# The first quad of self-attention: rows of x first on the load queue, weights in four pieces, normalisation ahead of the weight splits

## What is computed

```python
xn = layernorm(x)                       # per token, over 256
xq, xk, xv = xn @ wq.T, xn @ wk.T, xn @ wv.T      # 256 -> 1024 each
scores = softmax(xq.reshape(b, 16, s, 64) @ xk.reshape(b, 16, s, 64).T / 8)
x = x + (scores @ xv.reshape(b, 16, s, 64)) @ wo.T
```

## Time and profile before

| | |
|---|---|
| three runs | 1566.71, 1567.07 and 1562.39 us, median 1566.71 |
| the profiled execution | 1566.04 us, span 1564.3 us |
| time of it outside the span | 1.7 us |
| TensorE busy | 1434.1 us, 92% of the span |
| first matmul (transpose) of the span | 20.72 us |
| first projection matmul | 23.89 us |
| mean granted TensorE clock | 0.967 |

### The profile page before, as it was taken

One profiled execution on the slowest core, in us unless ns is written; L12 is line 12 of the kernel. 1 busy time (PEld: TensorE's weight loads), 2 busy tenths in 40 slices (PEclk: granted clock), 3 DMA queues, 4 the chain that ended last, 5 costly groups with the idle time before them and its releaser, 6 DMA issues. The chain is left out here.

```text
span 1564.3 us, 40213 instructions
## 1 busy us (share of the span) xinstructions
PE 1434.1 (92%) x12305; PEld 1241.7 (79%) x12305; DVE 967.4 (62%) x2473; ACT 763.7 (49%) x1879; POOL 682.0 (44%) x1060
## 2 busy tenths in 40 slices
PE   4999999999999999789999999999999369999997
PEld 3888878888888888668888888888887258888886
DVE  5747575757565656357777777777775235555553
ACT  4647474747464656236655655655655112222221
POOL 5434353535353535512355455465464523333332
PEclk9999999999999999789999999999999579999999
DMA  5606060707070707077667767767764235554451
GB/s 191 136 5 167 20 172 13 179 9 181 8 177 11 173 12 176 26 217 194 193 176 198 194 178 195 194 176 196 195 168 141 69 110 166 197 194 169 160 191 54
DMA packets 181964, 218.31 MB, mean 140 GB/s; under 512 B 83838, under 2 KB 150309, under 8 KB 181638
## 3 DMA queue, kind: packets, MB, share of 16 engines
q1 hardware_dynamic: 176360, 208.56, 48.1%
q0 software_dynamic: 3968, 6.59, 1.3%
q10 hardware_dynamic: 1568, 2.30, 0.5%
HBM read 138.67 MB, written 80.48 MB: 140 GB/s over the span
## 5 line engine op out<-in xcount | busy, mean ns | idle before, releaser
L1431 DVE TENSOR_REDUCE row_max<-psb_s 100x1 f32<-100x361 f32 x512 | 265.3, 530 | 140.1 <-PE psb_s L1654 135.0
L1305 ACT ACTIVATE probs<-psb_t 121x400 f32<-121x400 f32 (+1 forms) x384 | 190.4, 507 | 89.7 <-PE psb_t L1664 82.8
L1654 PE MATMUL psb_s<-k,q 97*100 97x362 f32 x512 | 185.0, 363 | 12.8 <-DVE row_max L1431 4.9
L519 POOL TENSOR_TENSOR diag<-neg_ident,row_max 100x400 fp32r<-100x400 f32 x128 | 112.8, 903 | 175.5 <-DVE row_max L612 146.7
L1664 PE MATMUL psb_t<-q,k 98*121 98x200 f32 (+1 forms) x768 | 148.5, 276 | 1.8 <-ACT probs L1305 1.8
L2144 PE MATMUL psd_h<-h_in,w_sb 128*128 128x256 f32 x640 | 144.0, 384 | 1.4 <-ACT h_in L2010 1.4
L2152 PE MATMUL psd_y<-w_sb,hid 128*128 128x256 f32 x640 | 144.5, 379 | 0.0
L2144 PEld LDWEIGHTS psd_h<-h_in,w_sb 128*128 128x128 f32 x640 | 123.3, 193 | 18.9 <-issue 1.8
L2152 PEld LDWEIGHTS psd_y<-w_sb,hid 128*128 128x128 f32 x640 | 120.1, 190 | 15.5
L1664 PEld LDWEIGHTS psb_t<-q,k 98*121 98x121 f32 (+1 forms) x768 | 126.8, 186 | 5.6 <-ACT probs L1305 2.5
L2025 ACT ACTIVATE hid<-psd_h,b_sb 128x256 f32<-128x256 f32 x100 | 47.4, 474 | 148.5 <-PE psd_h L2144 147.2
(11 more groups left out here) (230 smaller groups left out, 3710.0 us busy)
## 6 DMA issues: line engine op xcount, KB each, us to landing
w_sb<-in_w SPq DMA_DIRECT2D x40, 1024.0 KB, 7.6
routed_rows<-empty SPq DMA_DIRECT2D x7, 3855.0 KB, 18.7
packed_keys<-k_st SPq DMA_DIRECT2D x32, 724.0 KB, 4.1
k<-packed_keys SPq DMA_DIRECT2D x64, 362.0 KB
v_rows<-v_tok SPq DMA_DIRECT2D x32, 400.0 KB
v_ext<-v_rows SPq DMA_DIRECT2D x32, 400.0 KB
q<-packed_queries SPq DMA_DIRECT2D x64, 200.0 KB
k<-packed_keys SPq DMA_DIRECT2D x64, 181.0 KB
```

The lines of the kernel that those rows point to most:

```text
L519: pool.tensor_tensor(diag[:, g % 2], c.neg_ident[0:S, 0:S].unsqueeze(1).to_broadcast([S, GH, S]), row_max[:, g // 2 % 2, g % 2].unsqueeze( ...
L1305: act.activation(probs[0:KT[kt], u % 2, kt], ps_t[i % 2][0:KT[kt], 0:4 * S], ACT.Exp, scale=HD2 ** -0.5).then_inc(probs_ready, 1)
L1431: dve.reduce_max(row_max[:, p, h:h + 1], ps_s[h % 2][0:S, 0:S2], AX_X).then_inc(max_ready, 1)
L1654: pe.matmul(ps_s[h % 2][0:S, 0:S2E], q2[0:97, p, u, g, S * a:S * (a + 1)], k2[0:97, p, u, g], start=True, stop=True).then_inc(scores_ready, 1)
```

## The change

The diff below leaves nothing out but the mechanical replacement of the semaphores' names and counts for `wvT` and `woT` (their two low parts become four, one for each half). `piece_loaded[0]` and `[1]` are used again for `wvT` and `woT`.

```diff
+        PIECES = [(qk, half) for half in range(2) for qk in range(2)]
+        def columns(w, qk, half):
+            return w[:, qk, :, O1 // 2 * half:O1 // 2 * (half + 1)]
 # SP
             load_x(0, x_first)
-            sp.wait_ge(w_loaded[0], 16)
+            for n, (qk, half) in enumerate(PIECES):
+                first = O1 * qk + O1 // 2 * half
+                sp.dma_start(columns(w_stage, qk, half), wqkT[:, first:first + O1 // 2].rearrange(
+                    "(k p) n -> p k n", p=128)).then_inc(piece_loaded[n], 16)
             load_x(1, x_second)
             for i, w in ((2, wvT), (3, woT)):
-                sp.wait_ge(w_lo_ready, i - 1)
+                sp.wait_ge(w_lo_ready, i + 1)
 # ACT
-            for i, w in enumerate((wqkT[:, 0:O1], wqkT[:, O1:2 * O1])):
-                act.dma_start(w_stage[:, i], w.rearrange("(k p) n -> p k n", p=128)).then_inc(w_loaded[i], 16)
-            for i in range(2):
-                act.wait_ge(w_loaded[i], 16)
-                act.copy(w_hi[:, i], w_stage[:, i]).then_inc(w_hi_ready, 1)
+            def high_bits(n):
+                act.wait_ge(piece_loaded[n], 16)
+                act.copy(columns(w_hi, *PIECES[n]), columns(w_stage, *PIECES[n])).then_inc(w_hi_ready, 1)
+            high_bits(0)
+            high_bits(1)
             leading_bits(0)
+            high_bits(2)
+            high_bits(3)
 # POOL
-                pool.tensor_copy(w_hi[:, n + 2], w_stage[:, n]).then_inc(vo_hi_ready, 1)
-                pool.wait_ge(vo_hi_ready, n + 1)
-                pool.tensor_tensor(w_lo[:, n + 2], w_stage[:, n], w_hi[:, n + 2].bitcast(F32),
-                                   ALU.subtract).then_inc(vo_lo_ready, 1)
+                for half in range(2):
+                    hi, lo, src = columns(w_hi, n + 2, half), columns(w_lo, n + 2, half), columns(w_stage, n, half)
+                    pool.tensor_copy(hi, src).then_inc(vo_hi_ready, 1)
+                    pool.wait_ge(vo_hi_ready, 2 * n + half + 1)
+                    pool.tensor_tensor(lo, src, hi.bitcast(F32), ALU.subtract).then_inc(vo_lo_ready, 1)
 # DVE
+            def low_bits(n):
+                dve.wait_ge(w_hi_ready, n + 1)
+                hi, lo, src = (columns(t, *PIECES[n]) for t in (w_hi, w_lo, w_stage))
+                dve.tensor_tensor(lo, src, hi.bitcast(F32), ALU.subtract).then_inc(w_lo_ready, 1)
             moments(0)
-            low_bits(0)
             for i in range(QUAD):
                 normalize(0, i)
-            low_bits(1)
+            low_bits(0)
             trailing_bits(0)
+            for n in range(1, len(PIECES)):
+                low_bits(n)
 # PE
-                pe.wait_ge(xn_ready, q * QUAD + QUAD)
+                if not isinstance(q, int):
+                    pe.wait_ge(xn_ready, q * QUAD + QUAD)
                 for k in range(KD):
                     for i in range(QUAD):
+                        if isinstance(q, int) and k == 0:
+                            pe.wait_ge(xn_ready, q * QUAD + i + 1)
                         ins = pe.transpose(...)
+                if isinstance(q, int) and q == 0 and t % 4 == 0:
+                    pe.wait_ge(w_lo_ready, t // 2 + qk + 1)
-                    if f == FV and isinstance(q, int) and q == 0:
-                        pe.wait_ge(vo_lo_ready, 1)
+                    if f in (FV, FV + 1) and isinstance(q, int) and q == 0:
+                        pe.wait_ge(vo_lo_ready, f - FV + 1)
             turn_x(0)
-            pe.wait_ge(w_lo_ready, 2)
```

More of the change, by code:

```diff
@@ L202, in self_attention @@
         x_loaded = sem("x_loaded")
-        w_loaded = [sem(f"w_loaded{i}") for i in range(4)]
+        PIECES = [(qk, half) for half in range(2) for qk in range(2)]
+        piece_loaded = [sem(f"piece_loaded{n}") for n in range(len(PIECES))]
         w_hi_ready = sem("w_hi_ready")
@@ L313, in _ @@
             load_x(0, x_first)
-            sp.wait_ge(w_loaded[0], 16)
+            for n, (qk, half) in enumerate(PIECES):
+                first = O1 * qk + O1 // 2 * half
+                sp.dma_start(columns(w_stage, qk, half), wqkT[:, first:first + O1 // 2].rearrange(
+                    "(k p) n -> p k n", p=128)).then_inc(piece_loaded[n], 16)
             load_x(1, x_second)
             for i, w in ((2, wvT), (3, woT)):
-                sp.wait_ge(w_lo_ready, i - 1)
+                sp.wait_ge(w_lo_ready, i + 1)
                 sp.dma_start(w_stage[:, i % 2].rearrange("p k n -> p (k n)").rearrange(
                     "p (k n) -> p k n", n=w.shape[1]), w.rearrange("(k p) n -> p k n", p=128)
-                             ).then_inc(w_loaded[i], 16)
+                             ).then_inc(piece_loaded[i - 2], 16)
             for q in range(2, QUADS):
@@ L349, in cross_inputs @@
             def cross_inputs():
-                sp.wait_ge(vo_lo_ready, 2)
+                sp.wait_ge(vo_lo_ready, 4)
                 for dst, src in ((c.wk_st, cross["wk"]), (c.wv_st, cross["wv"]), (c.wq_sb, cross["wq"])):
@@ L439, in quad @@
                         if isinstance(q, int) and q == 0 and r - 2 < 2:
-                            act.wait_ge(vo_lo_ready, 2)
+                            act.wait_ge(vo_lo_ready, 4)
                         else:
@@ L469, in split_weights @@
             def split_weights(n):
-                pool.wait_ge(w_loaded[n + 2], 16)
-                pool.tensor_copy(w_hi[:, n + 2], w_stage[:, n]).then_inc(vo_hi_ready, 1)
-                pool.wait_ge(vo_hi_ready, n + 1)
-                pool.tensor_tensor(w_lo[:, n + 2], w_stage[:, n], w_hi[:, n + 2].bitcast(F32),
-                                   ALU.subtract).then_inc(vo_lo_ready, 1)
+                pool.wait_ge(piece_loaded[n], 32)
+                for half in range(2):
[3 more added lines that the diff above has]
+                    pool.tensor_tensor(lo, src, hi.bitcast(F32), ALU.subtract).then_inc(vo_lo_ready, 1)
             inverse_root(0)
@@ L479, in _ @@
             split_weights(1)
-            pool.wait_ge(vo_lo_ready, 2)
+            pool.wait_ge(vo_lo_ready, 4)
             pool.memset(c.mask_t, 0).then_inc(c.cross["mask_cleared"], 1)
@@ L779, in quad @@
                             if isinstance(q, int) and q == 0:
-                                pe.wait_ge(vo_lo_ready, 2)
+                                pe.wait_ge(vo_lo_ready, 4)
                             hi, lo = (t[:, i % 2] for t in (o_hi, o_lo))
```

## The result

The changed kernel takes **1557.01 us** (median of 11 runs, 1551.37 to 1560.1) against 1565.12 us for the kernel before, run beside it (11 runs, 1561.84 to 1567.48). The ratio is 0.9947, 95% interval 0.9932 to 0.9962: 8.1 us less, with an interval of about 6 to 10.6 us. The forecast was 1558.5 us (7.5 less). The profiled execution took 1555.15 us, span 1553.4.

A forecast was written before the change was run, and what follows sets the result against it. The late landing of x was taken to bound the kernel's start: first projection 8.3 us earlier, 0.8 given back before the fifth, so 7.5 us off the profiled 1566.04, giving 1558.5 us; 8-in-10 range 1554.5 to 1564.5.

The forecast's parts named there:

- The bound: Kernel start: x, 0.4 MB, not the 2 MB of weights, bounds it; issued first, x lands at 8.2 us, not 13.83.
- Statistics to the first projection: From x's landing: var_eps at 10.3, xn done 13.1, x_lo 15.45, first projection 15.6 us, 8.3 earlier than 23.89.
- The 1.84 us: Start, on POOL: without low_bits(0) beside it, var_eps takes 0.23 us instead of 2.07, which removes 1.84 us by itself.
- From the first projection to the fifth: Three low_bits on DVE delay the copies; fifth projection at 22.65 us (before 30.14), giving back 0.8 of 8.3 us.
- wvT, woT and POOL: Value fills: wvT's second half ready by 29.7 to 30.7, needed at 31.9 us; margin 1.2 us or more, no cost.
- The other margin: Next quad: POOL's inverse_root(1) ends at 38.2 to 40.3 us, DVE's normalize wants it at 41.3; 1 us left at worst.
- Rival B: POOL becomes the bound at the second value fill or next normalize: 3 to 5 us lost, 1562 to 1563 us; chance 0.10.
- The pieces and wvT: Weight loads: pieces 0 and 1 land by 11.1, needed by 12.7; wvT waits until 18.05 and lands at 23.1 us.
- The sum: Whole kernel: 8.3 - 0.8 = 7.5 us gained from the profiled 1566.04 us, giving 1558.5 us, 0.48% less.
- Rival A: Start: x lands at 11 to 13.8 us, not 8.2; 2.8 to 5.6 us lost, 1561.3 to 1564.1 us; chance 0.13.
- Rival C: First stage: new breaks keep TensorE at its low clock, up to 22 us lost, 1570 to 1578 us; chance 0.05.
- Rival D: Two later changes of stage: clock levels fall otherwise, 1561.5 to 1566 us despite full gain at the start; chance 0.10.

The follow-up runs named there:

- experiment 2: Kernel before, with both whole weight loads moved from ACT's queue to SP's, behind x; order of work unchanged: 1561.21 us, ratio 0.9973.
- experiment 4: Changed kernel, with the four weight pieces issued on ACT's queue beside x on SP's, second quad of x waiting for piece 1: 1556.09 us, ratio 0.9945.
- experiment 5: Changed kernel, but SP issues the weight pieces only when x has landed: 1557.05 us, ratio 0.9960.
- experiment 1: Kernel before, loads kept: normalize ahead of low_bits(0), low_bits(1) behind trailing_bits, transposes batch by batch: 1563.63 us, ratio 1.0002.
- experiment 6: Changed kernel with low_bits(0) put back ahead of normalize: 1560.37 us, ratio 0.9957.
- Experiment 7: Changed kernel plus 105 small warming matmuls (ratio 1.0034), 30 wide ones (0.9954), low parts of pieces 2 and 3 on POOL (0.9963), or the last two together (0.9960).
- the last experiments: Changed kernel plus wide warming matmuls and low parts of pieces 2 and 3 on POOL: 1556.28 us; with loads issued beside the constants too: 1553.51 us.

## Why the prediction was right

*The bound.* "x, 0.4 MB, is the bound of the start": experiments 2, 4 and 5 show it. x landed at 8.27 where the sum said 8.2. Alone, the load took 4.12 us against the 4.4 of the sum of 2.5 us that don't depend on size and 1.9 at the rate of the later x loads; the total is measured, the split between the two terms is not.

*Statistics to the first projection.* `var_eps` 10.41 (10.3), `xn` done 13.19 (13.1), `x_lo` done 15.49 (15.45), first projection 15.54 (15.6). The 1.84 us that the prediction ascribes to taking `low_bits(0)` from beside `var_eps` is real with the old loads: in experiment 1 `var_eps` took 0.24 us and not 2.07. With x early and pieces of half the size the same order is worth less, 0.9 us, and by way of `rstd` (experiment 6). The sum did not hang on it, since it added up the new order from its own start.

*From the first projection to the fifth.* Forecast 0.8 us given back, measured 0.43. The copies started at 18.92 and not at 19.2, since three `low_bits` took 3.49 us and not 3.6. That this stretch is paced by DVE was half the truth. The prediction had TensorE done with its four banks "by 21.5 to 23, depending on the clock", but counted only DVE's 22.65. Experiment 7 shows the lower clock as a second bound at nearly the same place, and in three kernels with the same work here it ended last and put the fifth projection 0.3 to 0.45 us later than in the changed one. That the profiled execution of the changed kernel had an early rise is luck, of that size.

*wvT, woT and POOL.* No wait of TensorE at the value fills, as forecast. The second half of wvT was ready at 29.72 (27.33 + 2.39), and the second value fill started at 31.78: 2.1 us of margin where I had 1.2 or more. The other margin, 1 us at worst, was 2.3: the next quad's `rstd` was ready at 38.55, and DVE's first `xn` started at 40.87. Rival B did not happen, and the last experiments show how near it is: with the fills 2.0 us earlier it takes more than half of the gain.

*The pieces and wvT.* Piece 1 landed at 11.18 (11.1), due at 12.7; wvT was issued at 17.78 (18.05) and landed at 22.75 (23.1).

*The sum.* 7.5 us forecast; 7.92 at the fifth projection, 8.0 at `diag`, 8.1 in the medians. Of the 1.5 us between the forecast time, 1558.5, and the measured one, 0.6 are the gain and 0.9 the base: the forecast counted from an execution of 1566.04 us, and the median beside the changed kernel was 1565.12. That the whole sum came within 0.6 us is partly luck, since neither the marks nor the medians are that sharp. Rival A (x not early) is refuted by the landing at 8.27. Rival C (the clock) did not happen; the weight loads were at the higher level from 19.4 us on. Rival D, the later stages falling otherwise, is there with a spread of 8 us, in either direction, and not only at the two changes of stage: up to 5 us of it lie within self-attention. It did not carry the median away.

## What to carry to other kernels

When a load is late, look at what was issued beside it and not only at its size: the small load that starts the longest chain goes first, with the big ones behind it on its queue and none beside it on another, and is issued before the set-up that it doesn't need. An early operand helps only if nothing that waits for a later one stands ahead of its use in an engine's order, so move the loads and the order together; here they gave 6.1 us together and 4.5 one by one. For a change worth half a per cent, read marks in the trace as well as medians, and find out first how much the rest of the kernel, and each mark, varies by itself.

## What had not been expected of the hardware

A subtraction on DVE of two on-chip operands held up POOL's `rstd` (1.97 us, not 1.05) as it had `var_eps`. POOL's operation had started 0.17 us after it and touches 4 columns.

22.7 us of matmuls 128 wide, one every 216 ns, left TensorE at the lower of its clock levels. Of the 30 matmuls 384 wide the last ones ran at the higher level; the row of their weight loads goes from 330 to 187 ns (shortest, median, longest):

```profile
L807 PEld LDWEIGHTS ps_ot<-ones_r x30: 187/330/333, 4.0 to 11.8; 128*128 128x128 f32 x30
```
